# Taking the warm-up matmuls on zeros out of a fused attention and expert-FFN kernel

## What is computed

```
x = x + attn(layernorm(x))      # 16 heads of 64, RoPE, causal softmax
x = x + ffn(layernorm(x))       # one of 8 experts is chosen per sequence

def attn(u):
    q, k, v = split(u @ W_qkv.T);  q, k = rope(q), rope(k)
    scores = q @ k.T / sqrt(64);   scores[above the diagonal] = -inf
    return softmax(scores) @ v  @ W_o.T
def ffn(u):
    z = layernorm(u) * ln_g + ln_b
    probs = softmax(batchnorm(mean over rows of z) @ Wr + br);  e = argmax
    return (relu(z @ W_down[e] + b_down[e]) @ W_up[e] + b_up[e]) * probs[e]
```

## Time and profile before

| | us |
|---|---|
| median of 2 runs | 5917.94 (5898.46 to 5937.41) |
| the profiled execution | 5901.22 |
| its span on the slowest core (core 5) | 5899.3 |
| spans of the eight cores | 5875.3 to 5899.3 |

### The profile page before, as it was taken

How to read it: one execution, slowest core, us unless ns; L and a number is a source line. 1 busy time by engine, 2 the same in 40 slices (tenths; PEclk the granted TensorE clock), 3 DMA queues, 4 the chain that set the end, 5 groups by cost and what they waited for, 6 DMA issues and landing times. The chain is left out here.

```text
span 5899.3 us, 50095 instructions; the slowest of 8 cores (5875.3 to 5899.3 us)
## 1 busy us (share of the span) xinstructions
PE 4128.1 (70%) x12804; PEld 1195.3 (20%) x12804; DVE 2246.7 (38%) x2561; ACT 1653.7 (28%) x1983; POOL 1415.1 (24%) x1736
## 2 busy tenths in 40 slices
PE   0166899985346799999335689999634679999833
PEld 0022222222112222222012222222201222222211
DVE  1144333334444333333434433333443443333344
ACT  0000455550000155553000035555000005555300
POOL 0018110002234600010340831000133370100034
PEclk9889666677569866667558977766756897667765
DMA  5410000002031000002021100000203100000101
GB/s 144 125 46 22 1 1 1 1 16 60 11 111 34 13 1 1 1 1 72 4 88 55 23 3 1 1 1 1 75 7 111 35 16 0 1 1 1 61 14 68
DMA packets 151786, 180.81 MB, mean 31 GB/s; under 512 B 89823, under 2 KB 110559, under 8 KB 151015
## 3 DMA queue, kind: packets, MB, share of 16 engines
q1 hardware_dynamic: 151532, 177.61, 9.9%
HBM read 133.54 MB, written 44.04 MB: 30 GB/s over the span
## 5 line engine op out<-in xcount | busy, mean ns | idle before, releaser
L640 ACT ACTIVATE PT<-pss,ecol_s 128x1024 bf16<-128x1024 f32 x1280 | 1379.0, 1112 | 1409.4 <-PE pss L612 1402.6
L571 DVE RECIPROCAL rb<-po 64x512 f32<-64x512 f32 x256 | 859.9, 3359 | 1835.3 <-PE po L561 1835.3
L612 PE MATMUL pss<-qkT 64*128 64x512 bf16 x2560 | 1032.5, 494 | 0.0
L657 POOL TENSOR_SCALAR_AFFINE_SELECT PT<-PT 128x128 bf16<-128x128 bf16 x1024 | 275.0, 292 | 2578.5 <-ACT PT L640 2577.7
L539 PE MATMUL po<-PT,v 128*65 128x512 bf16 (+3 forms) x2560 | 832.0, 463 | 1.6 <-POOL PT L657 1.2
L606 PE MATMUL pss<-ident_s 128*128 128x512 bf16 x1280 | 641.2, 501 | 18.6 <-POOL qkT L501 18.6
L471 PE MATMUL psq<-u1T,wqk 128*128 128x512 bf16 x2048 | 481.1, 378 | 222.3 <-DVE t1b L484 222.3
L561 PE MATMUL po<-lr,ones_s 1*64 1x512 f32 x512 | 375.5, 823 | 241.3 <-ACT lr L554 205.8
L879 PE MATMUL psz<-t,ones_s 128*1 128x512 f32 x256 | 225.0, 1033 | 368.0 <-DVE t L868 368.0
L497 POOL TENSOR_TENSOR t2b<-qks,ropeB_s 128x512 f32<-128x512 f32 x256 | 324.5, 1268 | 649.5 <-DVE t1b L484 613.3
L539 PEld LDWEIGHTS po<-PT,v 128*65 128x65 bf16 x2560 | 291.4, 136 | 611.3 <-issue 535.9
(11 more groups left out here) (100 smaller groups left out, 2541.9 us busy)
## 6 DMA issues: line engine op xcount, KB each, us to landing
xb<-x SPq DMA_DIRECT2D x64, 512.0 KB, 3.6
xr<-x SPq DMA_DIRECT2D x64, 512.0 KB, 3.6
out<-x2o SPq DMA_DIRECT2D x64, 512.0 KB, 2.6
wqk<-wqk_b SPq DMA_DIRECT2D x64, 256.0 KB, 3.0
cbuf_f<-wqk SPq DMA_DIRECT2D x16, 512.0 KB, 4.5
wvb<-wv_b SPq DMA_DIRECT2D x32, 256.0 KB
wob<-wo_b SPq DMA_DIRECT2D x32, 256.0 KB
wqk_b<-cbuf_b SPq DMA_DIRECT2D x16, 256.0 KB, 2.8
```

The costliest lines, as they stand in the source:

```text
L571: e.reciprocal(rb[sl][:, :], posb[sl][64:128, :])
L612: e.matmul(pss[sl2][:, (jj % 2) * 512: (jj % 2) * 512 + 512], qkT[hb:hb + 64, kcol + jj * 128: kcol + (jj + 1) * 128], qkT[hb:hb + 64, qco ...
L640: e.activation(PT[:, slot0 * 512: slot0 * 512 + 1024], pss[sl2][:, :], AF.Exp, bias=self.ecol[:, 1:2], scale=0.125) \
L657: e.affine_select(PT[:, col:col + 128], PT[:, col:col + 128], pattern=[[1, 128]], compare_op=ALU.is_ge, fill=0.0, base=0, channel_multipli ...
```

## The change

All three kinds of warm-up matmul go: the 12 at the start of `p1`, the 16 at the start of `p2a`, and the one ahead of each score pair. The wait for `qkT` moves from inside the first `_smm` of a sequence to an instruction of its own at the start of `p2a` on the same queue. All other work, its order and its buffers stay.

```diff
@@ p1
-                self.warm(psv[0][:, 0:512], 12)
@@ p2a
-            self.warm(pss6[:, 1024:1536], 16)
+            self.add("tensor", lambda e, w=self.qkT_base + NH * self.NQB:
+                     e.wait_ge(self.s_qkT.h, w))
@@
-                            w_head = (self.qkT_base + NH * NQB
-                                      if (h == 0 and qb == 0 and pl == 0)
-                                      else 0)
+                            w_head = 0
@@ _smm
                                 if wf:
                                     e.wait_ge(self.s_exp.h, wf)
-                                e.matmul(pss[sl2][:, 0:512],
-                                         self.ident[:, 0:128],
-                                         self.ident[:, 128:640],
-                                         start=True, stop=True,
-                                         skip_group_check=True)
                                 for jj in (j0, j0 + 1):
                                     e.matmul(pss[sl2][:, (jj % 2) * 512:
```

## The result

The changed kernel takes 5969.95 us (median of 11 runs, 5958.07 to 5996.26), the kernel before 5906.93 us in the same comparison (10 runs, 5898.02 to 5937.41). The ratio is 1.0103, 95% interval 1.0083 to 1.0122. It is a small, clear loss of 1%, or 63 us, where 544 us of gain were forecast.

The account below looks back on a forecast made before the run. Attention was taken as bound by PE, at 1.2 GHz more than half of the time. A head going from 44.7 to 36.2 us saves 8.5, times 64 = 544 us, from 5901 to 5355 us; range 5170 to 5630.

Parts of the forecast that it names:

- The bursts of 12 and 16 and the moved wait at 0: Start of p1 and p2a: removing the warm-up bursts and moving the qkT wait were each priced at 0.
- A group 1.10 us cheaper at 1.2 GHz: Attention on PE: without L606 a group's scores take 1.90 us for 3.00, bounds 0.86 and 1.28 saved.
- A head at 1.2 GHz of 45.7 us: Attention at the slow clock: a head falls from 56.7 to 45.7 us, 43.9 to 48.1 by the bounds.
- the clock never rises: Rival, attention: 6120 us with full switches kept, 5965 with 45.7 us a head; chance 0.09.
- A head at 2.4 GHz between 28.1 and 32.8, ACT then being the bound: Attention at the fast clock: PE needs 26.6 us, ACT is late; 30 us taken for a head.
- ACT's chain of 28.1: A head's lower bound at 2.4 GHz: 10 x 2.12 + 4 x (1.15 + 0.58) = 28.1 us on ACT.
- The clock decides: Attention: the share of a head's time at 2.4 GHz rises from 0.385 to 0.5 without the dummies.
- its sign of being wrong: Attention: wrong if the clock falls below 0.6, or groups at 1.2 GHz take over 3.9 us.
- With nine L606 in it the slow stretch stays slow: Slow 23.89 us of a head: PE 92% busy, 91% in the fast stretch, so busy is not enough.
- come right behind or in a run of four full PV matmuls: Clock rises at 1046.15 and 1080.28 tied to PV runs, which come closer without L606: 47% of a group for 36%.
- L606 multiplies zeros and gives nothing that the rows show.: Dummy ahead of each score pair: claimed to give nothing visible, supporting a share rising to 0.5 without it.
- the dummies hold the clock up for part of the time: Rival, attention: dummies fill PE's queue; share 0.15 to 0.3, 5755 to 5570 us; chance 0.15.

Follow-up runs that it names:

- the run at a share of 0.90 to 0.94: Scores padded to 128 rows with zeros, no dummies ahead of pairs, two 128-row dummies at each query block's end, against the kernel before: 4885.1 us, ratio 0.8271.

## Why the prediction was wrong

**The prices held.**
- *The bursts of 12 and 16 and the moved wait at 0*: 1.0009 without the bursts (0.9977 to 1.0041).
- *A group 1.10 us cheaper at 1.2 GHz*: 4.71 to 3.67 us, 1.04 saved; the last group with the block's end 7.10 to 5.91 (1012.89 to 1018.80), 1.19 saved.
- *A head at 1.2 GHz of 45.7 us*: 2918 / 64 = 45.6. The second rival, "the clock never rises", was put at 6120 us with the full switches kept, and at 5965 with 45.7 us a head; 5970 were measured. By the mean over all cores the head goes from 44.2 to 45.2 us, the same 1.0 us longer as from 44.7 to 45.7.
- *A head at 2.4 GHz between 28.1 and 32.8, ACT then being the bound*: the changed kernel never shows it, but the run at a share of 0.90 to 0.94 takes 28.5 us a head. ACT's chain of 28.1 was close: in that run a query block of three groups and its end take ACT 7.96 us (copy to copy, 867.64 to 875.60), where the chain gives 3 x 2.12 + 1.73 = 8.09. The 30 that I took is high for it. That run has 128-row scores and no row switches in its groups, so it supports the number for ACT and not the 26.6 for PE, which no run shows.

**The step that failed is "The clock decides".** It forecast that the share at 2.4 GHz would go from 0.385 to 0.5, and it went to 0; the clock of 0.50 in attention is also below the 0.6 that the prediction had named as its sign of being wrong. The inference had three parts.
- *"With nine L606 in it the slow stretch stays slow, so a full PE queue is not what brings the clock up here."* The last clause is right: 93% and 99% busy at 0.50 in two of the runs. What followed from it was that L606 has no part, and that is wrong: L606 differs from the score matmuls around it by its 128 rows. The same matmul on 64 rows gives 0.50, on 128 rows 0.68.
- *Both rises "come right behind or in a run of four full PV matmuls".* The first does; the second, at 1080.28, was misread. PE's timeline of the kernel before has it in the second dummy of a group, 1.7 us after the PV run has ended:

```profile
1076.83 1.92 PE L539 MATMUL po<-PT,v 128*65 128x512 bf16 x4
1078.54 0.63 PE L606 MATMUL pss<-ident_s 128*128 128x512 bf16 x1
1079.10 1.03 PE L612 MATMUL pss<-qkT 64*128 64x512 bf16 x2
1080.07 0.48 PE L606 MATMUL pss<-ident_s 128*128 128x512 bf16 x1
```

  The first rise, at 1046.15, lies in a dummy as well. In this core's first attention stage 26 of the 33 rises lie in a dummy, 7 in a score matmul and none in a PV matmul; on two of the eight cores more than a third of them lie in PV. So where a rise stands names no cause, and the PV rule rested on one of two rises. Every full run of PV in the kernel before also has an L606 right behind it, so its rows could not tell the two apart. In the changed kernel the runs of PV come every 3.67 us instead of every 4.71, and the clock does not rise.
- *"L606 multiplies zeros and gives nothing that the rows show."* The same matmul on 64 rows takes the clock to 0.50, so on 128 it gave the share of 0.38. With data in place of zeros the time is the same, 1.0006 (0.9958 to 1.0055), and the padded scores bring the clock up with half of their rows on zeros.

What I should have weighed is in the code and in the rows' shapes: of the eight useful matmuls of a group, four use half of the array's rows (`64*128`) and four all of them. Taking out two full-row matmuls lowers the part of full-row work, whatever it does to the spacing of PV. The rival that held this, "the dummies hold the clock up for part of the time", was priced from a share of 0.15 to 0.3, not at 0, and its mechanism had been put as "they fill PE's queue". The chance of 0.09 for no rise at all was too low for a quantity of which the forecast had one sample, at one mix.

**The sum, with the true share.** 1 / (1/45.7) = 45.7 us a head for 44.7 before, times 64: 64 us more, 5965. The gain at 1.2 GHz (11 us of a head that would have taken 56.7) and the loss of the stretches at 2.4 GHz nearly cancel, which is why the result looks like almost nothing.

**What stays open.** How much of the falls behind a query block's end is due to the 0.92 us of idle and how much to the one-row matmul was not separated; filling the idle time sufficed to take the share from 0.76 to 0.90. It is not shown either what the order of full-row and half-row matmuls does to the clock at the same length of a group, nor how the share follows from the mix: rows are shown to be the cause, and the size of their effect at each mix is only what the table has.

## What to carry to other kernels

Before a warm-up matmul is taken out or put in, count for each stretch how many of its matmuls use all 128 rows: with half-row matmuls in the mix PE was 99% busy here and stayed at 1.2 GHz. A matmul over 64 rows that is padded to 128 with zeros cost no more PE time here and lifted the clock, at the price of copies on an engine that had time for them; dummies lift it only at a price on PE's path, and pay where PE would stand idle. And where one unknown, here the share of time at 2.4 GHz, multiplies every other term, spread the chances over its whole range, its ends included.

## What the runs showed of the hardware

- The granted clock depends on the rows that matmuls use, and busy time alone does not raise it: 0.50 at 93% busy with 64-row dummies, 0.68 with 128-row ones, 0.50 at 99% busy in the changed kernel with its ends filled. Where all matmuls of a group use 128 rows, filling idle time does raise it, 0.88 to 0.95.
- Neither the values (0.69 in the first stage with zeros in the kernel without bursts and 0.69 with data) nor the columns of the array (a share of 0.37 over all cores with 64 of 128, 0.38 with all) matter much.
- A score matmul costs the same on 64 and on 128 rows: four of them 1.88 and 1.89 us at 1.2 GHz. A switch between kinds with different rows adds 0.11 to 0.14 us to the distance of starts (behind four PV matmuls the scores start after 1.85 us at 1.2 GHz, a 128-row dummy on 128 columns after 1.71). Without such switches a group of ten matmuls at 2.4 GHz takes 2.17 us, with four of them 2.59. Rows are not all of it: a 128-row dummy on 64 columns also starts only after 1.85 us.
